# Attention's softmax maxima: computed one and three eighths of a unit ahead, and turned one key tile later

## The reference

```
x: [4, 1024, 256]; 16 heads of 16
qkv = layernorm(x) @ qkv_w.T + qkv_b
scores = einsum('bhqd,bhkd->bhqk', q, k) / 4
attn   = softmax(scores, axis=-1)
out    = einsum('bhqk,bhkd->bhqd', attn, v)
x = x + layernorm(out @ out_w.T + out_b)
```

## Time and profile before

| | us |
|---|---|
| median of 3 runs (2083.22 to 2085.46) | 2083.36 |
| the profiled execution | 2075.49 |
| its span | 2073.3 |
| PE / DVE / ACT / POOL busy, share of the span | 96% / 73% / 62% / 29% |
| mean granted TensorE clock | 0.979 |

### The profile page before, as it was taken

How to read it: one execution, slowest core, us unless ns; L and a number is a source line. 1 busy time by engine, 2 the same in 40 slices (tenths; PEclk the granted TensorE clock), 3 DMA queues, 4 the chain that set the end, 5 groups by cost and what they waited for, 6 DMA issues and landing times. The chain is left out here.

```text
span 2073.3 us, 42107 instructions
## 1 busy us (share of the span) xinstructions
PE 1988.5 (96%) x16914; PEld 1404.6 (68%) x16914; DVE 1519.1 (73%) x2466; ACT 1287.6 (62%) x2561; POOL 600.0 (29%) x480
## 2 busy tenths in 40 slices
PE   7999999999999999998999999999999999489997
PEld 6743333333333347987888888888888888378996
DVE  7889999999999978897646464646464644468774
ACT  3248888888888877776444445454545454256663
POOL 2200000000000014455334343434343433125454
PEclk9979999999999999999999999999999999789999
DMA  6832232223223222416212221212122212232221
GB/s 230 252 60 66 54 81 59 71 62 78 65 61 84 61 76 77 124 41 174 73 63 93 63 92 63 92 63 93 64 92 63 92 63 83 72 111 83 103 113 72
DMA packets 103491, 180.66 MB, mean 87 GB/s; under 512 B 24233, under 2 KB 65857, under 8 KB 98177
## 3 DMA queue, kind: packets, MB, share of 16 engines
q1 hardware_dynamic: 103296, 177.97, 28.1%
HBM read 138.48 MB, written 38.67 MB: 85 GB/s over the span
## 5 line engine op out<-in xcount | busy, mean ns | idle before, releaser
L741 DVE TENSOR_REDUCE att_sb_mx<-att_ps_psM 128x1 f32<-128x1024 f32 x512 | 624.4, 1221 | 26.9 <-PE att_ps_psM L980 23.3
L1194 ACT ACTIVATE att_sb_pt<-att_ps_psSO 128x512 f32<-128x512 f32 x1024 | 556.8, 597 | 94.6 <-PE att_ps_psSO L998 39.7
L980 PE MATMUL att_ps_psM<-stack_sb_k,stack_sb_q 48*128 48x512 f32 x1024 | 381.9, 454 | 5.0 <-DVE att_sb_mx L741 2.6
L998 PE MATMUL att_ps_psSO<-stack_sb_q,stack_sb_k 50*128 50x512 f32 x1024 | 373.3, 444 | 0.0
L1010 PE MATMUL att_ps_psSO<-att_sb_pt,stack_sb_v 128*32 128x256 f32 x4096 | 326.4, 391 | 8.6 <-ACT att_sb_osb L1187 8.6
L998 PEld LDWEIGHTS att_ps_psSO<-stack_sb_q,stack_sb_k 50*128 50x128 f32 x1024 | 153.1, 185 | 201.8 <-ACT att_sb_pt L1194 155.5
L1010 PEld LDWEIGHTS att_ps_psSO<-att_sb_pt,stack_sb_v 128*32 128x32 f32 x4096 | 82.0, 108 | 192.1 <-issue 102.5
L2317 ACT ACTIVATE glag_sb_sg<-att_ps_psM 128x512 f32<-128x512 f32 x64 | 38.3, 598 | 249.1 <-PE att_ps_psM L2077 249.0
L2544 DVE TENSOR_TENSOR glan_sb_dm<-att_ps_psSO,glan_sb_dm 128x512 f32<-128x512 f32 x128 | 82.2, 684 | 126.6 <-PE att_ps_psSO L2197 126.6
L980 PEld LDWEIGHTS att_ps_psM<-stack_sb_k,stack_sb_q 48*128 48x128 f32 x1024 | 156.8, 189 | 19.3 <-DVE att_sb_mx L741 16.4
L2681 POOL TENSOR_TENSOR glan_sb_dm<-glan_sb_dm,glaa_sb_masked 128x1024 f32<-128x1024 f32 x64 | 156.1, 2460 | 19.1 <-DMA glan_sb_dm<-decay_rows 19.1
(11 more groups left out here) (306 smaller groups left out, 4833.4 us busy)
## 6 DMA issues: line engine op xcount, KB each, us to landing
glan_sb_dm<-decay_rows SPq DMA_DIRECT2D x32, 1024.0 KB, 5.1
qk_parts<-stack_sb_part SPq DMA_DIRECT2D x32, 512.0 KB, 3.3
glai_sb_eg<-decay_exp SPq DMA_DIRECT2D x64, 256.0 KB, 6.1
moe_sb_gb<-gate_rows SPq DMA_DIRECT2D x8, 2048.0 KB, 7.7
stack_sb_q<-qk_parts SPq DMA_DIRECT2D x192, 64.0 KB, 3.0
stack_sb_k<-qk_parts SPq DMA_DIRECT2D x96, 128.0 KB, 4.4
att_sb_rb<-sums SPq DMA_DIRECT2D x32, 256.0 KB
attended<-att_sb_on SPq DMA_DIRECT2D x32, 256.0 KB, 4.9
```

The lines of the kernel that those rows point to most:

```text
L741: nc.vector.tensor_reduce(mx[:, qh, 8 * r + c:8 * r + c + 1], psM[:, t % 2, :], AX.X, ALU.max).then_inc(maxima_taken, 1)
L980: mm = pe.matmul(psM[:, t % 2, c * ST:(c + 1) * ST], q[rs, g, qh, j, n * P:(n + 1) * P], k[rs, g, j, c * ST:(c + 1) * ST], start=True, sto ...
L998: pe.matmul(psS[:, ring_slot(pos), :], k[rs, g, j, s * P:(s + 1) * P], q[rs, g, qh, j, :], start=True, stop=True).then_inc(ring_done, 1)
L1194: nc.scalar.activation(pt[:, s % (LAG + 2), ORDER[i], :], psS[:, (pos + 1) % 3, :], ACT.Exp, scale=AD ** -0.5).then_inc(ring_taken, 1)
```

## The change

`AHEAD` becomes `TILES // 2 - 2` = 6 and `TURN_AT` becomes 6. The wait for the queries and keys of the unit after next moves with the tiles, from s = 4 to s = 5.

```
-        AHEAD = TILES // 2
-        TURN_AT = 5
+        AHEAD = TILES // 2 - 2
+        TURN_AT = 6
...
                         if s == TURN_AT and not final:
                             pe.wait_ge(ring_taken, HG * (KT * u + s) - 2)
                             turn_rows(u + 1, ring_slot(HG * s))
-                        if s == KT // 2 and not last:
+                        if s == (TILES - AHEAD) // 2 and not last:
```

## The result

| | us |
|---|---|
| before, median of 5 runs | 2083.22 |
| after, median of 5 runs | 2157.07 |
| ratio, 95% interval | 1.037 (1.035 to 1.039) |
| predicted | 2120.6, range 2102 to 2133 |

The change makes the kernel 74 us slower; I had forecast 37. One of the five runs of after, the profiled one, took 3833 us with PE slow in every stage, those of no change too; so the profile is of another execution of the same kernel, 2173.93 us long (span 2171.8, mean clock 0.947), in a series with a median of 2155.5 us. It is the longest of its series of six, which goes down to 2132.5 us (clock 0.964); an execution of 2154.8 us had a clock of 0.957, before has 0.979. So the profile shows more of the loss than the median does.

A forecast was written before the change was run, and what follows sets the result against it. PE, DVE and ACT were all taken as near their end in the attention stage. Waits +39.2, prologue -2.0 and unit 30 +0.05 gave +37.2 us on 2083.4: 2120.6 us, range 2102 to 2133.

The forecast's parts named there:

- What bounds the stage: Attention stage: PE busy 98.6%, DVE 96.7%, ACT 88.5%, so none of them gives back a wait put in.
- The rows land with the spread read that is queued ahead of them: SP's queue: the next unit's rows land about 0.5 us behind the reciprocals' transfer, making each unit start 1.35 us late.
- 6.50 us from turn to release: Start of a unit: reciprocals in 6.00 us behind the turn, rows 0.5 us later; 5.15 us left, so 1.35 us late.
- My bound from below: Landing of the rows: with nothing ahead, 1.4 us after issue, 2.6 us behind the turn, and nothing would wait.
- Which units: Attention stage: units 2 to 30 wait for their rows, 29 in all; units 1 and 31 don't.
- Prologue: Before the first score: two tiles less, first score about 2.5 us earlier, taken as -2.0 us because of the clock.
- unit 30: Two tiles more beside pairs that had none: +0.05 us; the projection's later wait for all maxima costs nothing.
- SP's queue: Loads behind the rows would end at 312.9 us, still ahead of the den transfer at 313.95: no cost.
- the wait at +39.2 us: Starts of units in the attention stage: 29 units, each 1.35 us late, all of it on the path.
- the clock at 1.00 in the stage: Sign expected in the profile after: the granted clock stays full, 1.00, in the attention stage.
- the wait also costs the clock or the restart: Rival, attention stage: clock falls for one or two pairs of each unit, 35 us more, 2156 us; chance 0.05.
- 1.8 for all: Start of each waiting unit: PE idles some 1.8 us (1.35 + 0.41) once in 21.6 us.

## Why the prediction was wrong, point by point

- **What bounds the stage: right.** PE, DVE and ACT are all near their end, and no wait put in was given back: in the changed kernel units at the full clock took 20.27 us plus their wait (20.98 for a start 0.72 late, 21.21 for 0.93).
- **The rows land with the spread read that is queued ahead of them: right**, and now shown by four runs: rows first, read earlier, read halved, read doubled. I took 6.50 us from turn to release, it was 6.36; the wait per unit was 1.22 instead of 1.35 us, 34 instead of 39 us. My bound from below, rows alone on the queue, was 2.6 us behind the turn; with nothing ahead of them the first score came 2.96 to 3.03 us behind it.
- **Which units: right**, 29; one of them (the one turned at the low clock) had no wait left.
- **Prologue, unit 30, SP's queue: right.** 2.3 us won at the first score; and with the changed numbers and the rows first nothing was lost behind that, neither at the end of the stage nor by the loads.
- **The step that failed is the missing term for the clock.** The sum has the wait at +39.2 us and nothing for a lower clock behind it ("the clock at 1.00 in the stage"); the clock in the stage was 0.90, and the falls cost some 42 us in the execution of 2154.8 us and 59 to 61 us in the profiled one. I had it as the rival "the wait also costs the clock or the restart", to which I gave 0.05, with the argument that the low level is seen only in the prologue, where PE waits at every tile. Its 2156 us beside the measured 2157 are luck in part: it had one or two slow pairs in each of 29 units, and the runs showed 7 to 48 us at the low clock behind 8 of 28 waits and none behind the others. The trace of before could not refute it: in the stage where the wait was to come, the weight loads never sat idle for more than 0.7 us at a time, so a clock of 1.00 there said nothing about an idle time of 1.8 us. I had counted a missing observation as one against.
- **And the spread of the waits was left out.** The mean idle time at the start of a unit, 45.8 / 28 = 1.64 us, lies below every one behind which the clock fell; the late units of the spread did it, with idle times up to 3.26 us. Such a unit costs up to 11 us beyond its wait (33.91 us from turn to turn with a wait of 2.85), nine times the mean wait, and the clock stayed low through the next unit, which had no wait at all and took 29.27 us. The spread was there to be read in the trace of before: POOL starts 5.28 to 7.00 us behind the turn. The latest is the second unit of rows 6, 570.96 us, whose turn was here:

```profile
563.96 0.28 PE L1018 MATMUL att_ps_psSO<-att_sb_ident,att_sb_mparts 128*32 128x128 f32 x1
```

An estimate from it, with the distance of 0.38 us and the start at 5.14: 7.00 + 0.38 - 5.14 = 2.24 us late, an idle time of some 2.65 us on the weight loads, where the forecast had 1.8 for all.

Still open: what decides whether a wait of 1.9 to 2.6 us on the weight loads makes the clock fall. Equal waits did and didn't, in the run with AHEAD alone (1.92) and in the one with two reads (2.33); one of 2.58 didn't. So which units were hit is not explained, only what their falls cost.

## What to carry to other kernels

When a small transfer is moved later, look at what is issued ahead of it on its queue: here its landing was that transfer's, not its own, and issuing it first cost nothing. A new wait of TensorE that comes back regularly has two prices, its length and the clock behind it; the second can be the larger, and an idle time longer than any in the trace of before is an open question, to be held in the range. And read the spread of a landing, not only its mean.

## What the runs showed of the hardware

- In the changed kernel the clock fell behind idle times of 1.85 to 3.26 us on the weight loads (0.48 us less on the matmuls where the timeline shows both, 2.72 and 2.24), which came once per unit of 20 us, and stayed low for some 7 to 48 us although PE had work at once. With an idle time of 0.7 us per unit (AHEAD = 4, rows first) it stayed at 1.00 in the stage.
- At 1.2 GHz a pair took 2.16 us, at 2.4 GHz 1.23: the time does not double. If PE's part of a pair doubles at the low clock, it is 1.08 us at the full one (an estimate, half of 2.16), less than the 1.22 us that DVE needs for its tile; then DVE sets the pace at the full clock and PE at the low one. No run shows this by itself.
- The 256 KB that four rows give to 128 partitions had landed for POOL 5.9 us after their issue on average in the kernels before and after (4.8 to 7.0 in single units), 5.0 where the rows were issued 3 us behind them (the turn alone) and 6.7 where the rows were ahead; half of it came 2.5 us earlier.
- In the changed kernel two small DMAs (8 KB each) queued behind that read released PE 0.2 to 0.6 us behind POOL's start; with nothing ahead of them they landed at most 1.3 us after the second one's issue (367.49 against 366.23). The Trainium skill, DMA: Bandwidth & Descriptors, section on queues, rings and completion order, says that a semaphore's increment lands only after every earlier write of its DMA engine. The 28 waits of the changed kernel agree: each ended behind POOL's start. No run shows the order on one engine.
